# First experts of a two-layer kernel: 37 of 39 row tiles turned by VectorE in 32 by 32 blocks instead of by TensorE

## What is computed

```python
assign = jnp.argmax(x @ centroids.T, axis=1)
for e in range(8):
    h = _layernorm(xs, ln_g[e], ln_b[e])
    h = jax.nn.relu(h @ w1[e].T + b1[e])      # 256 -> 1024
    ye = xs + h @ w2[e].T + b2[e]             # 1024 -> 256
    y = y + jnp.where((es == e)[:, None], ye, 0.0)
out = alpha * y + (1.0 - alpha) * xs
```

## Time and profile before

| | |
|---|---|
| median of 3 runs | 1062.14 us (1060.17 to 1065.8) |
| profiled execution | 1063.0 us |
| its span, first to last instruction | 1061.2 us |
| mean granted TensorE clock | 0.942 |
| busy over the span: PE / DVE / ACT / POOL | 91% / 59% / 46% / 36% |

### The profile page before, as it was taken

One profiled execution on the slowest core, in us unless ns is written; L12 is line 12 of the kernel. 1 busy time (PEld: TensorE's weight loads), 2 busy tenths in 40 slices (PEclk: granted clock), 3 DMA queues, 4 the chain that ended last, 5 costly groups with the idle time before them and its releaser, 6 DMA issues. The chain is left out here.

```text
span 1061.2 us, 29656 instructions
## 1 busy us (share of the span) xinstructions
PE 963.9 (91%) x11001; PEld 824.6 (78%) x11002; DVE 624.7 (59%) x1458; ACT 489.6 (46%) x1332; POOL 383.5 (36%) x341
## 2 busy tenths in 40 slices
PE   6899999789999999999987999999766798999996
PEld 3466666788999999999966777777655687999995
DVE  3478877863445445445413788888986676344442
ACT  2656665204454454454346777777552440222221
POOL 0435344421222222221203555555662001355552
PEclk9999999989999999999998999999866659899999
DMA  9874571575222222222055656666421711344441
GB/s 337 248 296 126 130 244 49 180 266 145 83 93 87 84 88 89 82 89 70 8 114 86 126 120 140 146 130 125 95 71 56 305 63 41 124 136 139 132 134 34
DMA packets 133006, 135.54 MB, mean 128 GB/s; under 512 B 73868, under 2 KB 122126, under 8 KB 130724
## 3 DMA queue, kind: packets, MB, share of 16 engines
q1 hardware_dynamic: 121668, 90.80, 30.9%
q0 software_dynamic: 11232, 43.27, 12.9%
HBM read 96.21 MB, written 44.77 MB: 133 GB/s over the span
## 5 line engine op out<-in xcount | busy, mean ns | idle before, releaser
L990 PE MATMUL psall<-rows 128*128 128x128 f32 x1872 | 226.0, 278 | 2.0 <-DVE rows L1044 2.0
L990 PEld LDWEIGHTS psall<-rows 128*128 128x128 f32 x1872 | 219.3, 195 | 2.6 <-issue 2.5
L957 POOL DMA_INDIRECT x<-ffn_rows,tok_i x78 | 82.1, 1053 | 247.6 <-DVE rows L1063 146.5
L1002 PE MATMUL psall<-whi,rows 128*128 x624 | 141.0, 379 | 0.0
L1044 DVE COPY rows<-wlo 128x2048 f32 (+1 forms) x78 | 75.1, 963 | 110.5 <-PE psall L990 108.9
L1002 PEld LDWEIGHTS psall<-whi,rows 128*128 128x128 f32 x624 | 115.7, 190 | 14.1
L1301 DVE STREAM_TRANSPOSE whi<-whi 32x512 f32<-32x512 f32 x128 | 89.8, 701 | 9.0 <-POOL whi L1264 7.7
L1103 ACT ACTIVATE rows<-psall,rows 128x128 f32<-128x128 f32 x312 | 84.9, 383 | 12.1 <-PE psall L990 7.4
L1382 ACT ACTIVATE whi<-psall 32x512 f32<-32x512 f32 x128 | 75.2, 587 | 29.5 <-PE psall L1511 26.6
L962 POOL DMA_INDIRECT attn_rows<-rows,tok_i x39 | 39.5, 1013 | 120.2 <-DVE rows L1076 120.2
L1254 POOL TENSOR_TENSOR whi<-whi,cst 128x512 f32<-128x512 f32 x32 | 40.6, 1270 | 94.3 <-ACT whi L1382 94.3
(11 more groups left out here) (233 smaller groups left out, 1697.9 us busy)
## 6 DMA issues: line engine op xcount, KB each, us to landing
ffn_rows<-mod_rows SPq DMA_DIRECT2D x2, 4096.0 KB
wlo<-in_W SPq DMA_DIRECT2D x2, 4096.0 KB, 17.5
whi<-in_w SPq DMA_DIRECT2D x5, 1024.0 KB, 6.7
whi<-mod_rows SPq DMA_DIRECT2D x4, 1024.0 KB, 14.3
ffn_rows<-rows SPq DMA_DIRECT2D x8, 512.0 KB
ffn_rows<-x SPq DMA_DIRECT2D x8, 512.0 KB
wlo<-attn_rows SPq DMA_DIRECT2D x32, 128.0 KB, 3.5
v_turn<-wlo SPq DMA_DIRECT2D x32, 128.0 KB, 3.1
```

What stands on the lines that cost most here:

```text
L957: eng.indirect_dma_start(xin[j % DEEP], None, src_d, bass.IndirectOffsetOnAxis(tok_i[:, j:j + 1].bitcast(U32), 0), bounds_check=T, oob_is_ ...
L990: last = eng.matmul(b_up[t.par][f // 4][:, (f % 4) * P:(f % 4 + 1) * P], w_now[:, c, f * P:(f + 1) * P], inT[t.par][:, c * P:(c + 1) * P], ...
L1002: last = eng.matmul(b_dn[t.par][:, 0:D], hidT[t.par][:, f * P:(f + 1) * P], w_down[:, bass.ds(e, 1), f, :].rearrange("p o n -> p (o n)"), ...
```

## The change

In layer 0 tiles 0 and 1 are still turned by TensorE. For the other 37 tiles VectorE turns the rows with 16 block transposes, each of 32 partitions by 64 elements, into one of three buffers (`turned`). ScalarE's `act_in` then reads that buffer and not PSUM. The blocks of tile s are turned in step s, eight behind the weight copy and eight behind `out_rows`. All other stages of layer 0 have a lag two steps larger, so that the turning is two tiles ahead. SyncE's later loads wait for `inT` in place of `tin`. The second expert stage keeps its order. The three uses of `Chain` on VectorE share one semaphore, which leaves one for the new signal `tb`.

```diff
             def after(self, n):
-                return not self.static or self.j >= n
+                return self.j >= n if self.static else n < NTILE
...
+            turned = [vs[:, i * D:(i + 1) * D] for i in range(2)] + [extra[:, 0:D]]
+            by_pe, ahead = (2, 2) if normed else (NTILE, 0)
...
             def on_sync(eng):
-                eng.wait_ge(e_["tin"], 3)
+                eng.wait_ge(e_["inT"], 3)
...
                 def turn_in(t):
+                    if t.after(by_pe):
+                        return
...
-                pipeline(eng, [(0, turn_in), (1, up), (2, down)], head)
+                pipeline(eng, [(ahead, turn_in), (ahead + 1, up), (ahead + 2, down)], head)
...
                 def act_in(t):
-                    eng.wait_ge(e_["tin"], t.j + 1)
+                    if t.after(by_pe):
+                        eng.wait_ge(e_["tb"], t.j - by_pe + 1)
+                    else:
+                        eng.wait_ge(e_["tin"], t.j + 1)
...
-                    prep_in(eng, e, inT[t.par], b_in).then_inc(e_["inT"], 1)
+                    prep_in(eng, e, inT[t.par], turned[t.third] if t.after(by_pe) else b_in).then_inc(e_["inT"], 1)
...
-                pipeline(eng, ([(3, rstd)] if normed else []) + [(0, act_in), (1, act_hidden)], head)
+                pipeline(eng, ([(ahead + 3, rstd)] if normed else []) + [(ahead, act_in), (ahead + 1, act_hidden)], head)
...
+                def turn_blocks(half):
+                    def stage(t):
+                        if not t.after(by_pe):
+                            return
+                        if half == 0:
+                            eng.wait_ge(s_in[t.slot], (t.rounds + 1 + rounds_before[t.slot]) * 16)
+                            if t.after(by_pe + 3):
+                                eng.wait_ge(e_["inT"], t.j - 2)
+                        to = turned[t.third].rearrange("p (c i t) -> p c i t", c=C, i=4)
+                        rows_in = xin[t.slot][:, 0:D].rearrange("p (c q d) -> p c q d", c=C, q=4)
+                        for i in (2 * half, 2 * half + 1):
+                            for q in range(4):
+                                last = eng.transpose(to[32 * q:32 * q + 32, :, i, :], rows_in[32 * i:32 * i + 32, :, q, :])
+                        if half:
+                            last.then_inc(e_["tb"], 1)
+                    return stage
...
-                pipeline(eng, [(0, fetch_weights)] + ([(3, norm_rows)] if normed else []) + [(2, out_rows)], head)
+                if normed:
+                    pipeline(eng, [(ahead, fetch_weights), (0, turn_blocks(0)), (ahead + 3, norm_rows), (ahead + 2, out_rows), (0, turn_blocks(1))], head)
+                else:
+                    pipeline(eng, [(0, fetch_weights), (2, out_rows)], head)
```

More of the change, by code:

```diff
@@ L155, in end @@
                 self.base, self.n, self.off = self.base + self.n * times, 0, 0
+        dve = {}
         def settle(eng):
@@ L351, in attn0_vector @@
         def attn0_vector(eng):
-            ch = Chain(eng, "s_va")
+            ch = dve["chain"] = Chain(eng, "s_va")
             eng.memset(zeros, 0.0).then_inc(s_z, 1)
@@ L870, in plan0_vector @@
         def plan0_vector(eng):
-            ch = Chain(eng, "s_vp")
+            ch = dve["chain"]
             eng.wait_ge(ev["key"], B)
@@ L898, in __init__ @@
                 self.j, self.par, self.pairs = i * DEEP + at, at % 2, i * (DEEP // 2) + at // 2
-                self.slot, self.rounds = at % DEEP, i + at // DEEP
+                self.slot, self.rounds, self.third = at % DEEP, i + at // DEEP, at % 3
                 self.static = isinstance(i, int)
             def after(self, n):
-                return not self.static or self.j >= n
+                return self.j >= n if self.static else n < NTILE
         def pipeline(eng, stages, head, count=NTILE):
@@ L935, in expert_stage @@
             nbank = nf * P // 512
-            names = "tin inT w up act dn y sum" + (" b bs mv ln rs out" if normed else "")
+            names = "tin inT w up act dn y sum" + (" tb b bs mv ln rs out" if normed else "")
             e_ = {n: sem(f"{tag}_{n}") for n in names.split()}
@@ L1279, in _ @@
                 f0_vector(eng)
-                ch = Chain(eng, "s_vc")
+                ch = dve["chain"]
                 for v in vp[0:2]:
```

## The result

The changed kernel takes 1083.26 us (median of 4 runs, 1080.24 to 1083.69) against 1061.31 for the one before: ratio 1.0186, 95% interval 1.0161 to 1.0212. The forecast was 1080.5. (On the first 16 blocks the prediction has only "XX". They ran from 238.32 to 242.30, before the copy at 243.17.)

A forecast was written before the change was run, and what follows sets the result against it. TensorE bounds the kernel at 7.25 us a tile; after the change VectorE would, at 3.91 + 16 x 0.245 = 7.83 us. The 18.4 us loss on the 1062.14 median gives 1080.5 us, range 1066 to 1098.

The forecast's parts named there:

- The bound: First expert stage: TensorE sets the pace at 7.25 us a tile, 0.22 of it transposes, 8.1 us over 37 tiles.
- The present step: VectorE's work per tile before the change: weight copy 1.14, norm 0.41, `out_rows` 2.36, sum 3.91 us.
- The price p: Time between starts of successive block transposes on VectorE, 0.245 us, scaled from layer 1's 32x512 transposes.
- the lower bound: Least p, from overlapping VectorE statistics instructions scaled to 64 elements: 0.126 us.
- The sum: VectorE's step becomes 3.91 + 16 x 0.245 = 7.83 us against TensorE's 7.03; over 34 steps the loss is 18.4 us.
- the rule on the drain: Trainium skill: a VectorE instruction starts only after the one ahead leaves the pipe; by it alone p is 0.232, +11.5 us.
- the formula: Loss in us at the first expert stage for a given p: 34 x (3.91 + 16p) - 247.8.
- TensorE's wait: `up` waits for the weight copy some 0.8 us a tile from about the fifth, near 25 us in all.
- What is moved: The gather, wanted by VectorE two steps behind `sum` instead of TensorE four behind: no cost, 5 us margin.
- Rival 1: VectorE hides the blocks: p = 0.126, step 5.93 us, TensorE stays the bound, 8.1 us gained, 1054; chance 0.12.
- Rival 3: Further waits in VectorE's step, such as 0.3 us per copy (1091), or p = 0.28 (1100); chance beyond forecast range 0.06.
- Rival 4: TensorE, 90% busy, drops its clock: up to 7 us more a tile, whole stage over 1300 us; chance 0.02.

The follow-up runs named there:

- lags only: The changed kernel's lags and semaphores, but TensorE turns all 39 tiles and VectorE none: 1061.66 us, ratio 1.0001 to the kernel before.
- 20 blocks: The changed kernel with 4 more block transposes a tile, written to a place nobody reads: 1129.16 us, one run.

## Why the prediction was right

1. **The bound.** TensorE set the pace at 7.25 us, and the transposes were on the path: in the five runs with VectorE relieved and no transposes on TensorE the period is 7.03, 0.22 less, as the earlier trace rows gave it.
2. **The present step, 3.91 us.** Measured 7.86 less the blocks' 1.98 + 2.02, 3.86: the norm holds up what follows for 0.33 and not 0.41, and the first block behind `out_rows` starts 0.21 and not 0.18 after the last statistics instruction.
3. **The price p.** 0.245 forecast, 0.249 measured, duration 0.235 for "near 0.23". The number was right and its reason incomplete. I took it as a property of the instruction kind, with the fixed 0.18 us paid by all. It belongs to blocks that change their group of partitions; those that don't start 0.126 us apart, which is the lower bound to the digit. The row chosen, layer 1's transposes, also changes both groups each time, and so it was the right row. That was luck: the row was chosen for its kind, and nothing in the prediction looked at the partitions.
4. **The sum.** The copy of tile 37 was forecast for 522.98 and started at 524.43; the loss there is 19.9 us for 18.4. From the copy of tile 3 at 256.40 (0.36 sooner than forecast) that is 268.03 / 34 = 7.88 us a step for 7.83. The mis-sized term is 16p, 4.00 us for 3.92, partly made good by the norm's 0.08; each turn of the loop adds about 0.1 us (a step of 7.98 for 7.87), the entry into it 0.35, which stayed hidden while VectorE waited for TensorE. Two side sums are slightly off: with p = 0.232, by the rule on the drain, the formula gives +11.3 us and not +11.5, and with p = 0.21 -0.6 and not -0.7.
5. **TensorE's wait,** near 25 us forecast, is 21.8 in the waits.
6. **What is moved** was free (lags only, 1.0001; no wait for a gather behind the first), and so was ScalarE's other source.
7. **The rivals.** Rival 1 asked for p below 0.196. It is what happens when groups don't change, or with half the blocks, and gives 1053 to 1055 where the prediction had 1054. Rival 3's further waits exist, but as some 0.02 us a step. Rival 4 did not occur at 92% busy. It did with 20 blocks: TensorE was busy 191 of 236 us, its granted clock there was 0.96, and 0.66 from 330 to 340 us, behind an idle stretch of 4.5 us. The `up` there took 6.11 us for 3.83, but ended at 338.90, before the next weight copy at 340.44 asked for it. What I had not thought of is the loop body's size: it would have cost 14 us with four blocks more.

## What to carry to other kernels

Taking work off the bounding engine pays only while the step of the engine that takes it, summed from the starts of its instructions and not from busy time, stays below; here VectorE looked half idle and had 3.3 us free in 7.25, for 4.0 of new work. For many short VectorE instructions price the distance of their starts, and look whether source and target begin in the same 32 partitions as those ahead. When the new work doesn't fit, see what else the second engine does that a third could: moving one copy turned a loss of 1.9% into a gain of 0.8%. (Turning two tiles side by side, so that two blocks in a row share both groups, would bring the mean distance near 0.19 us by the starts measured above, (0.205 + 0.169) / 2, an estimate; it was not tried.)

## What the runs showed of the hardware

- Block transposes of 32x64 float32 start 0.126 us apart when source and target start in the same 32 partitions as those of the one ahead (0.169 right behind a held one), 0.249 when either changes.
- A VectorE loop body of 276 instructions a turn (as the trace counts them) had a gap of some 3.3 us at each turn from the second on and 23 packets of instruction loads, one of 264 no gap and 5 packets.
- ScalarE copies 128x2048 float32 from SBUF to SBUF in 1.91 us, VectorE in 1.23.
- A float32 transpose of 128x128 costs TensorE 0.11 us in a stream of matmuls, though its record is 0.27 long.
